# Attention with a position bias: score stacks of 64 rows for pairs of heads, two heads alternating on the halves of TensorE's rows, and all causal masks for the maxima on VectorE

## The chip, the cores and the metric

One core of a Trainium2 chip runs the whole program. Its engines run side by side and meet at semaphores: TensorE (PE; PEld is its weight load, which overlaps the matmuls), VectorE (DVE), ScalarE (ACT), GpSimd (POOL) and SyncE (SP), which here only issues DMAs. The metric is device time in microseconds, the median of repeated executions.

## What is computed

The input is `x` of 16 batches, 512 tokens and 256 features; there are 16 heads of 16 features. For each batch, with `xn` the layer norm of `x`:

```python
qkv = xn @ w_qkv.T + b_qkv                       # q, k, v of 16 heads
att = einsum('bhqd,bhkd->bhqk', q, k) / sqrt(16)
att = att + bias[h, q - k]                       # cosine features of the position, a constant for some heads
att = softmax(where(causal, att, -inf))
attn = einsum('bhqk,bhkd->bhqd', att, v) @ w_proj.T + b_proj
y    = bf16(fp8(bf16(xn)) @ fp8(kernel)) + bias_ffn
out  = x + attn + y
```

## The kernel before, in words

The fp32 operands are split into a rounded part (hi) and a rest (lo), and a product is hi·hi + hi·lo + lo·hi. For the scores this is done in one matmul, by stacking operands in rows: `STK` holds for each head 48 rows of q or k parts (three products of 16 features) and 48 rows of position features (again three products), and on the query side two more rows with the negated row maximum, in two parts. So a score tile is one matmul of 96 rows, and a transposed one, for the exponentials, one of 98.

A batch `b` is worked in four groups `g` of four heads. A group has 11 slots `k`. In slot `k` TensorE makes one bank of transposed scores of group `g` (`scores_T`, L586, banks `scoreT_a` to `_c`), which ScalarE turns into `probs` by exp (L801), and one bank of plain scores of the group two ahead (`scores`, L565, banks `score_a` to `_c`), of which VectorE takes the row maxima (`chunk_max`). Both kinds have three banks, so the matmuls of slot `k` wait until the bank of slot `k-3` is read. The bank widths: four slots of 512 columns, four of 384, then two slots that hold two heads of 256 columns each and one with four heads of 128. For the first eight slots VectorE adds the mask and takes the maximum in one custom operation on each bank (L882, followed by a read of the accumulator); for the last three TensorE has added the mask with bf16 matmuls (L561, L569), and VectorE only reduces (L878).

When a group's maxima are there, TensorE transposes them (`job_MT`, L543), ScalarE writes the rounded part (L730) and VectorE the rest (L887), and SP sends both rows into `STK`, before that group's transposed scores begin.

All other work is hung into the slots by tables of (group, slot), in `V_AT` to `MT_AT`: the v projection (V), transposes of the next batch's `xn` (T), its q and k projections (QK), the fp8 product (FF), the output projection (PJ), probabilities times values (PV, L597, with its output on 32 columns of the array for each head) and the maxima (MT). `DVE_LAG` says how many slots later VectorE reads the result. The eight PSUM banks are full: three and three, and `misc_a`, `misc_b` for all other jobs. GpSimd masks the diagonal blocks of `probs` (L1089). Each engine executes its own list strictly in this order.

## Time and profile before

| | before |
|---|---|
| median of 3 runs | 870.61 us (869.99 to 874.59) |
| the profiled execution, its own time | 878.46 us |
| its span | 876.7 us |
| mean granted TensorE clock | 0.967 of 2.4 GHz |
| PE busy | 812.9 us, 93% |
| DVE busy | 648.6 us, 74% |
| ACT busy | 553.7 us, 63% |
| POOL busy | 470.9 us, 54% |
| DMA: share of 16 engines, bytes | 49%, 90.68 MB |

The span is the time from the first to the last instruction in the trace. A matmul's row shows its whole latency, so neighbouring matmuls overlap in the rows; what one costs the engine is the distance from its start to the next one's start. The same holds for VectorE's rows, which overlap by some 0.08 us.

### The profile page before, as it was taken

Reading aid. Unit: us, or ns where it says so; the run is one execution under the profiler, and the core shown is the slowest. Engines: PE = TensorE matmul, PEld = TensorE weight load, DVE = VectorE, ACT = ScalarE, POOL = GpSimd, SP = SyncE. Lnnn points to the kernel's source line nnn. Section 1 sums busy time; section 2 is a strip of 40 time slices with the busy share of each in tenths; the row PEclk is TensorE's granted clock in tenths of the full one; section 3 lists DMA queues with packets and bytes.
Section 4 is the critical chain, followed back from the end, with each engine's and each line's share of the span. In section 5 each row is a group of like instructions: output and inputs, shape, how many; then the busy total and the mean of one; then the engine's idle time right before and its main releaser. Section 6 shows DMA issues by size and latency. Waiting matters only on the chain.

```text
span 876.7 us, 21490 instructions
## 1 busy us (share of the span) xinstructions
PE 812.9 (93%) x5934; PEld 594.9 (68%) x5936; DVE 648.6 (74%) x1660; ACT 553.7 (63%) x1097; POOL 470.9 (54%) x485
## 2 busy tenths in 40 slices
PE   6699999999999998999999999999999999999983
PEld 3376676768677776867667586766768677776762
DVE  5976587787778878777787777777787778877732
ACT  4165576666767666675776577566666757766571
POOL 8533645546564654646475464645546464655442
PEclk9698799999999999999999999989999999999996
DMA  7834534464554455355445535653464554445312
GB/s 190 157 80 84 107 78 80 122 109 105 111 118 95 99 114 101 99 110 127 98 87 125 89 99 110 128 100 62 125 109 102 111 121 95 99 88 103 74 45 80
DMA packets 72453, 90.68 MB, mean 103 GB/s; under 512 B 18160, under 2 KB 38256, under 8 KB 72432
## 3 DMA queue, kind: packets, MB, share of 16 engines
q1 hardware_dynamic: 71360, 88.92, 48.2%
q10 hardware_dynamic: 1072, 1.51, 0.8%
q8 instruction: 9, 0.15, 0.1%
q14 instruction: 12, 0.10, 0.0%
HBM read 18.81 MB, written 8.91 MB: 32 GB/s over the span
## 4 chain that ended last, share of the span: by engine, by line
PE 57%; DVE 12%; SPq 9%; issue 8%; DMA 6%; ACT 5%; DVEq 1%; POOL 1%; ACTq 0%; POOLq 0%
PE misc_b L493 10%; PE misc_b L597 9%; PE misc_a L493 8%; SPq L272 8%; PE scoreT_b L586 6%; PE scoreT_a L586 4%; PE score_c L565 4%; PE score_a L565 4%; DMA stacks<-neg_max_T 4%; PE score_b L565 4%; PE scoreT_c L586 3%; DVE row_max L878 2%; ACT qk_parts L726 2%; DVE score_c L882 2%; DVE qk_parts L866 1%
## 5 line engine op out<-in xcount | busy, mean ns | idle before, releaser
L1089 POOL TENSOR_SCALAR_AFFINE_SELECT probs<-probs 128x512 f32<-128x512 f32 x256 | 160.2, 635 | 320.1 <-ACT probs L801 319.9
L801 ACT ACTIVATE probs<-scoreT_a 128x512 f32<-128x512 f32 (+1 forms) x240 | 135.3, 564 | 89.9 <-PE scoreT_a L586 89.4
L801 ACT ACTIVATE probs<-scoreT_b 128x512 f32<-128x512 f32 (+1 forms) x240 | 134.5, 561 | 85.0 <-PE scoreT_b L586 85.0
L882 DVE CUSTOM_DVE_ANT_0 score_a<-score_a,causal_mask_q 128x512 f32<-128x512 f32 (+1 forms) x176 | 112.8, 641 | 86.2 <-PE score_a L565 86.0
L801 ACT ACTIVATE probs<-scoreT_c 128x512 f32<-128x512 f32 (+1 forms) x224 | 125.6, 561 | 47.8 <-PE scoreT_c L586 47.7
L882 DVE CUSTOM_DVE_ANT_0 score_b<-score_b,causal_mask_q 128x384 f32<-128x384 f32 (+1 forms) x176 | 112.7, 640 | 43.8 <-PE score_b L565 28.4
L597 PE MATMUL misc_b<-probs,v_ones 128*32 128x128 f32 (+3 forms) x1536 | 120.8, 457 | 0.0
L586 PE MATMUL scoreT_b<-stacks 98*128 98x128 f32 (+3 forms) x368 | 105.2, 343 | 14.8 <-DMA stacks<-neg_max_T 14.1
L565 PE MATMUL score_a<-stacks 96*128 96x512 f32 (+3 forms) x336 | 108.4, 363 | 3.9 <-DVE row_max L882 2.6
L586 PE MATMUL scoreT_a<-stacks 98*128 98x512 f32 (+3 forms) x336 | 108.4, 369 | 1.7 <-ACT probs L801 1.5
L565 PE MATMUL score_b<-stacks 96*128 96x128 f32 (+3 forms) x368 | 108.8, 349 | 0.2 <-DVE row_max L882 0.2
L882 DVE CUSTOM_DVE_ANT_0 score_c<-score_c,causal_mask_q 128x512 f32<-128x512 f32 (+1 forms) x160 | 101.6, 635 | 3.8 <-PE score_c L565 3.3
L597 PEld LDWEIGHTS misc_b<-probs,v_ones 128*32 128x32 f32 x1536 | 46.5, 114 | 79.9 <-issue 71.2
L565 PE MATMUL score_c<-stacks 96*128 96x512 f32 (+3 forms) x320 | 99.9, 354 | 0.7 <-DVE row_max L882 0.7
L586 PE MATMUL scoreT_c<-stacks 98*128 98x512 f32 (+3 forms) x320 | 98.0, 355 | 0.6 <-ACT probs L801 0.6
L586 PEld LDWEIGHTS scoreT_b<-stacks 98*128 98x128 f32 x368 | 61.8, 193 | 27.4 <-DMA stacks<-neg_max_T 16.4
L565 PEld LDWEIGHTS score_a<-stacks 96*128 96x128 f32 x336 | 63.8, 198 | 12.5 <-DVE row_max L882 8.2
L882 DVE DVE_READ_ACCUMULATOR2_ANT row_max<- 128x1 f32 x512 | 71.9, 141 | 0.0
L565 PEld LDWEIGHTS score_b<-stacks 96*128 96x128 f32 x368 | 67.5, 198 | 3.8 <-DVE row_max L882 0.7
L586 PEld LDWEIGHTS scoreT_a<-stacks 98*128 98x128 f32 x336 | 57.5, 194 | 13.1 <-issue 6.1
L1078 POOL TENSOR_TENSOR quant_work<-quant_work 128x1024 f32<-128x1024 f32 x16 | 38.0, 2374 | 50.5 <-DVE quant_work L928 50.5
L565 PEld LDWEIGHTS score_c<-stacks 96*128 96x128 f32 x320 | 60.8, 198 | 4.2 <-DVE row_max L882 2.0
(234 smaller groups left out, 1824.9 us busy)
## 6 DMA issues: line engine op xcount, KB each, us to landing
stacks<-qk_parts SPq DMA_DIRECT2D x502, 96.0 KB, 2.8
x_ring<-in_L_attn_x SPq DMA_DIRECT2D x16, 512.0 KB, 3.9
attn<-out_T SPq DMA_DIRECT2D x64, 128.0 KB, 2.6
xn<-recips SPq DMA_DIRECT2D x31, 256.0 KB
out<-x_ring SPq DMA_DIRECT2D x15, 512.0 KB, 3.0
stacks<-neg_max_T SPq DMA_DIRECT2D x128, 8.0 KB, 1.8
stacks<-probs SPq DMA_DIRECT2D x16, 96.0 KB, 3.3
denominators<-out_T SPq DMA_DIRECT2D x64, 8.0 KB
```

Source lines behind the costliest of these rows:

```text
L272: eng.dma_start(STK[0:K_QK, g, a, h, :].bitcast(F32), QKP[r:r + HD, g // 2, :, a, :].bitcast(F32)) \
L493: last = mm(o, l(ct), r(ct), start=(ct == 0 and i == 0), stop=(ct == CT - 1 and i == 2))
L565: last = mm(SB_[n % 3][:, o:o + w], STK[0:K_SCORE, g, 0, h, P * qt:P * qt + P], STK[0:K_SCORE, g, 1, h, 0:w], start=(qt != 0), stop=(qt >= ...
L586: last = mm(bank[:, w * i:w * i + w], STK[0:K_ALL, g, 1, h, P * j:P * j + P], STK[0:K_ALL, g, 0, h, P * j:T], start=True, stop=True)
L597: last = mm(bank[32 * i:32 * i + 32, P * j:T], VA[:, j, HU * g + i, :, :].rearrange("p d a -> p (d a)"), probs(g, j)[:, i, :], start=(j == ...
L726: A(qk_part(m, 0), misc_of("QK", m)[:, :].unsqueeze(1).broadcast_to([P, 2, T]), ACT.Identity, bias=BQ[:, bias:bias + 1]).then_inc(qh_ready, 1)
L801: A(probs(g, j)[:, h0:h0 + nh, :], STB[(SLOTS * g + k) % 3][:, 0:nh * WJ[j]] .rearrange("p (h n) -> p h n", h=nh), ACT.Exp).then_inc(exp_d ...
L866: V.scalar_tensor_tensor(out=qk_part(m, 1), in0=misc_of("QK", m)[:, :], scalar=BQ[:, bias:bias + 1], in1=qk_part(m, 0)[:, 0, :].bitcast(F3 ...
L878: V.tensor_reduce(MX[:, g % 2, h0:h0 + nh, qt], bank.rearrange("p (h w) -> p h w", h=nh), AX_X, ALU.max).then_inc(max_done, 1)
L882: V.tensor_tensor_reduce(bank, bank, CMQ[:, T - w:T], 1.0, LEAST, ALU.add, ALU.max, MX[:, g % 2, h0, qt:qt + 1]).then_inc(max_done, 1)
L1078: GP.tensor_tensor(QT, QT, QM, ALU.add).then_inc(qr_done, 1)
L1089: GP.affine_select(out=d, in_=d, compare_op=ALU.is_ge, fill=0.0, base=0, pattern=[[0, HU], [1, P]], channel_multiplier=-1).then_inc(mask_d ...
```

## The change

- **Stacks.** A head has 64 rows: three products of q and k parts, and one row of rounded position features for each of the 16 features (`ROWS = 4` in `QKP`). Two heads stand one above the other, in rows 0 to 63 and 64 to 127 of `STK`. One DMA moves a pair (512 KB), two a group, where there were eight.
- **Low parts.** The small products of the features, and for groups 0 and 1 the two rows of maxima, stand in `EXT` (34 rows a head), and the transposed scores of these two groups get a second matmul that adds them (L602). The plain scores, whose maxima only shift the exponents, leave the low parts out. In groups 2 and 3 the bias is a constant, its parts fill spare rows, and the maxima replace two rows of `STK`.
- **Order.** `in_turn` alternates the matmuls of `scores_T` and `scores` within a slot. The transposed scores are of head `k % 4`, the plain ones of head `k % 4 ^ 1`, so the two stand on different halves of the rows.
- **Slots.** A group has 12: the last four hold for one head the tiles of 256 and 128 columns. The job tables are set anew.
- **Maxima.** The masks on TensorE are gone; VectorE's custom operation does every tile. VectorE splits the maxima into two parts before the transpose (`max_parts`, two small operations), so that ScalarE alone evacuates the transposed maxima.
- GpSimd has three waits for its masks in a group instead of four, with as many operations. The setup makes the constant rows and the low features in another way.

```diff
-PRODS = 3
-K_QK = PRODS * HD
-K_SCORE = 2 * K_QK
-K_ALL = K_SCORE + 2
-SLOTS = 11
-CHUNKS = 11
+PAIRS = H // 2
+ROWS = 4
+EXTRA = 34
+SLOTS = 12
+CHUNKS = 12
...
-SLOT_PLAN = [(0, h, 1) for h in range(4)] + [(1, h, 1) for h in range(4)] + [(2, 0, 2), (2, 2, 2), (3, 0, 4)]
-LAST_SLOT = [3, 7, 9, 10]
-PE_MASKED = (0, 1)
-CHUNK_PLAN = [(3, h, 1) for h in range(4)] + [(2, h, 1) for h in range(4)] + [(1, 0, 2), (1, 2, 2), (0, 0, 4)]
-V_AT = [(0, 3), (0, 4)]
-T_AT = [(0, 5), (0, 7)]
-QK_AT = [(0, 10), (1, 1), (1, 6), (2, 5)]
-FF_AT = [(2, 7), (2, 8)]
-PJ_AT = [(3, 3), (3, 6)]
-PV_AT = [(1, 2), (2, 2), (3, 2), (0, 2)]
-MT_AT = [(0, 1), (1, 3), (2, 3), (3, 1)]
+LAST_SLOT = [3, 7, 11]
+QUERY_TILES = [(3,)] * 4 + [(2,)] * 4 + [(1, 0)] * 4
+V_AT = [(0, 5), (0, 7)]
+T_AT = [(0, 9), (0, 9)]
+QK_AT = [(0, 11), (1, 1), (1, 7), (2, 9)]
+FF_AT = [(2, 7), (2, 7)]
+PJ_AT = [(3, 5), (3, 9)]
+PV_AT = [(1, 3), (2, 3), (3, 3), (0, 3)]
+MT_AT = [(0, 1), (1, 5), (2, 5), (3, 1)]
 ACT_LAG = {"T": 0, "QK": 0, "FF": 0, "MT": 0}
-DVE_LAG = {"V": 0, "T": 1, "QK": 1, "PJ": 0, "MT": 1}
+DVE_LAG = {"V": 0, "T": 1, "QK": 1, "PJ": 0}
 OUT_AT = 3
 AH_AT = [(2, 1), (2, 2)]
-INVERT_AT, LAST_INVERT_AT, DIVIDE_AT = (0, 10), (3, 7), (1, 10)
-STATS_AT, NORM_AT = (2, 6), [(3, 5), (3, 6), (3, 7), (3, 9)]
+INVERT_AT, LAST_INVERT_AT, DIVIDE_AT = (0, 11), (3, 8), (1, 10)
+STATS_AT, NORM_AT = (2, 7), [(3, 5), (3, 6), (3, 7), (3, 10)]
...
-        STK = sb("stacks", [P, G, 2, HU, T], F32R)
+        STK = sb("stacks", [P, PAIRS, 2, T], F32R)
+        EXT = sb("low_features", [P, PAIRS // 2, 2, T], F32R)
...
-        QKP = sb("qk_parts", [P, 2, PRODS, 2, T], F32R)
+        QKP = sb("qk_parts", [P, 2, ROWS, 2, T], F32R)
...
+        def rows_of(h):
+            return slice(64 * (h % 2), 64 * (h % 2) + 64), h // 2
+        def max_rows(g, h):
+            o, u = 64 * (h % 2), (HU * g + h) // 2
+            if g < 2:
+                return EXT[o + 32:o + 34, u, 0, :].bitcast(F32)
+            return STK[o + 11:o + 16:4, u, 0, :].bitcast(F32)
+        def send_max(eng, g):
+            for h in range(HU):
+                eng.dma_start(max_rows(g, h), MTS[2 * TT * h:2 * TT * h + 2 * TT, g % 2, :].bitcast(F32)) \
+                    .then_inc(max_loaded[g], 16)
...
-                for a in range(2):
-                    for h in range(HU):
-                        stack_part(sp, g, h, a)
+                for u in (2 * g, 2 * g + 1):
+                    r = 32 * (u % 4)
+                    sp.dma_start(STK[:, u, :, :].bitcast(F32), QKP[r:r + 32, u // 4, :, :, :].bitcast(F32)) \
+                        .then_inc(stack_loaded[g], 16)
             def load_max(b, g):
                 sp.wait_ge(mts_ready, 4 * b + g + 1)
-                for part in range(2):
-                    sp.dma_start(STK[K_SCORE + part:K_SCORE + part + 1, g, 0, :, :].rearrange("o h n -> o (h n)").bitcast(F32),
-                                 MTS[:, g % 2, part, :].bitcast(F32)).then_inc(max_loaded[g], 16)
+                send_max(sp, g)
...
             def job_MT(b, g):
-                pe.wait_ge(max_done, ROW * b + SLOTS * (g + 1))
+                pe.wait_ge(mh_done, 4 * b + g + 1)
                 bank = misc("MT", (g - 1) % G, b if g else b - 1)
-                nc.tensor.transpose(bank[0:HU * TT, 0:P], MX[:, g % 2, :, :].rearrange("p h t -> p (h t)"),
+                nc.tensor.transpose(bank[0:HU * 2 * TT, 0:P],
+                                    MXP[:, g % 2, :, :, :].rearrange("p h i t -> p (h i t)").bitcast(F32),
                                     IDF[:, :]).then_inc(mt_ready, 1)
             def scores(b, g, c, early=False):
-                qt, h0, nh = CHUNK_PLAN[c]
-                w = P * (qt + 1)
                 n = CHUNKS * g + c
+                rows, u = rows_of(HU * g + (c % 4 ^ 1))
                 if c == 0:
-                    if isinstance(b, int) and b == 0:
-                        pe.wait_ge(feat_loaded[g], 16 * (2 * HU if g < 2 else HU))
-                    pe.wait_ge(stack_loaded[g], 128 * (b + 1))
-                if n >= 3:
+                    pe.wait_ge(stack_loaded[g], 32 * (b + 1))
+                if n >= 3 or not early:
                     pe.wait_ge(max_done, ROW * b + n - 2)
-                elif not early:
-                    pe.wait_ge(max_done, ROW * b - [1, 0, 2][n])
-                if qt == 0:
-                    mm(SB_[n % 3][:, :].rearrange("p (h w) -> p h w", h=nh), CMT[:, :],
-                       IDB[:, :].unsqueeze(1).broadcast_to([P, nh, P]), start=True, stop=False)
-                for i in range(nh):
-                    h, o = h0 + i, w * i
-                    last = mm(SB_[n % 3][:, o:o + w], STK[0:K_SCORE, g, 0, h, P * qt:P * qt + P],
-                              STK[0:K_SCORE, g, 1, h, 0:w], start=(qt != 0),
-                              stop=(qt >= 2 or (qt == 0 and i == nh - 1)))
-                    if qt == 1:
-                        last = mm(SB_[n % 3][:, o + P:o + w], CMT[:, :], IDB[:, :], start=False, stop=True)
-                last.then_inc(s_ready, 1)
+                o = 0
+                for qt in QUERY_TILES[c]:
+                    w = P * (qt + 1)
+                    last = mm(SB_[n % 3][:, o:o + w], STK[rows, u, 0, P * qt:P * qt + P], STK[rows, u, 1, 0:w],
+                              start=True, stop=True)
+                    o += w
+                    if qt == QUERY_TILES[c][-1]:
+                        last.then_inc(s_ready, 1)
+                    yield
             def scores_T(b, g, k, first):
-                j, h0, nh = SLOT_PLAN[k]
-                w = WJ[j]
+                n = SLOTS * g + k
+                rows, u = rows_of(HU * g + k % 4)
+                extra = slice(rows.start, rows.start + EXTRA)
                 if k == 0:
-                    pe.wait_ge(max_loaded[g], 32 * (b + 1))
-                n = SLOTS * g + k
-                if n >= 3:
+                    if isinstance(b, int) and b == 0 and g < 2:
+                        pe.wait_ge(feat_loaded[g], 64)
+                    pe.wait_ge(max_loaded[g], 64 * (b + 1))
+                if n >= 3 or not first:
                     pe.wait_ge(exp_done, ROW * b + n - 2)
-                elif not first:
-                    pe.wait_ge(exp_done, ROW * b - [1, 0, 2][n])
-                bank = STB[n % 3]
-                for i in range(nh):
-                    h = h0 + i
-                    last = mm(bank[:, w * i:w * i + w], STK[0:K_ALL, g, 1, h, P * j:P * j + P],
-                              STK[0:K_ALL, g, 0, h, P * j:T], start=True, stop=True)
-                last.then_inc(st_ready, 1)
+                tiles = [k // 4] if k < 8 else [2, 3]
+                o = 0
+                for j in tiles:
+                    bank = STB[n % 3][:, o:o + WJ[j]]
+                    o += WJ[j]
+                    last = mm(bank, STK[rows, u, 1, P * j:P * j + P], STK[rows, u, 0, P * j:T], start=True, stop=(g >= 2))
+                    if g < 2:
+                        yield
+                        last = mm(bank, EXT[extra, u, 1, P * j:P * j + P], EXT[extra, u, 0, P * j:T],
+                                  start=False, stop=True)
+                    if j == tiles[-1]:
+                        last.then_inc(st_ready, 1)
+                    yield
+            def in_turn(*streams):
+                streams = list(streams)
+                while streams:
+                    streams = [x for x in streams if next(x, streams) is not streams]
...
-            def max_hi(b, g):
+            def max_T(b, g):
                 act.wait_ge(mt_ready, 4 * b + g + 1)
-                A(MTS[:, g % 2, 0, :], misc_of("MT", (g - 1) % G)[0:HU * TT, 0:P], ACT.Copy, scale=-1.0).then_inc(mh_done, 1)
+                A(MTS[:, g % 2, :], misc_of("MT", (g - 1) % G)[0:HU * 2 * TT, 0:P], ACT.Copy, scale=-1.0).then_inc(mts_ready, 1)
...
             def chunk_max(b, g, c):
-                qt, h0, nh = CHUNK_PLAN[c]
-                n = CHUNKS * g + c
-                w = P * (qt + 1)
-                bank = SB_[n % 3][:, 0:nh * w]
-                if qt in PE_MASKED:
-                    dve.wait_ge(s_ready, ROW * b + n + 1)
-                    V.tensor_reduce(MX[:, g % 2, h0:h0 + nh, qt], bank.rearrange("p (h w) -> p h w", h=nh),
-                                    AX_X, ALU.max).then_inc(max_done, 1)
-                else:
-                    wait_alone(dve, (x_loaded, 16), (s_ready, ROW * b + n + 1))
-                    V.tensor_tensor_reduce(bank, bank, CMQ[:, T - w:T], 1.0, LEAST, ALU.add, ALU.max,
-                                           MX[:, g % 2, h0, qt:qt + 1]).then_inc(max_done, 1)
-            def max_T(b, g):
-                dve.wait_ge(mh_done, 4 * b + g + 1)
-                V.scalar_tensor_tensor(out=MTS[:, g % 2, 1, :], in0=misc_of("MT", (g - 1) % G)[0:HU * TT, 0:P],
-                                       scalar=-1.0, in1=MTS[:, g % 2, 0, :].bitcast(F32),
-                                       op0=ALU.mult, op1=ALU.subtract).then_inc(mts_ready, 1)
+                n, h, o = CHUNKS * g + c, c % 4 ^ 1, 0
+                wait_alone(dve, (x_loaded, 16), (s_ready, ROW * b + n + 1))
+                for qt in QUERY_TILES[c]:
+                    w = P * (qt + 1)
+                    bank = SB_[n % 3][:, o:o + w]
+                    o += w
+                    last = V.tensor_tensor_reduce(bank, bank, CMQ[:, T - w:T], 1.0, LEAST, ALU.add, ALU.max,
+                                                  MX[:, g % 2, h, qt:qt + 1])
+                last.then_inc(max_done, 1)
+            def max_parts(b, g):
+                dve.wait_ge(max_done, ROW * b + CHUNKS * (g + 1))
+                V.tensor_copy(MXP[:, g % 2, :, 0, :], MX[:, g % 2, :, :]).then_inc(mx_hi, 1)
+                dve.wait_ge(mx_hi, 4 * b + g + 1)
+                V.tensor_tensor(MXP[:, g % 2, :, 1, :], MX[:, g % 2, :, :], MXP[:, g % 2, :, 0, :].bitcast(F32),
+                                ALU.subtract).then_inc(mh_done, 1)
...
```

In the rows of the order below, as in the whole text, names after the arrow are what is read. First TensorE at the start of group 0, before: slot 0, then slot 1, transposed scores and plain scores of whole 98 and 96 rows.

```order
L586 MATMUL scoreT_a<-stacks 128x512
L554 REGISTER_ALU
L557 REGISTER_ALU
L565 MATMUL score_b<-stacks 128x512
L586 MATMUL scoreT_b<-stacks 128x512
L557 REGISTER_ALU
L565 MATMUL score_c<-stacks 128x512
```

The same place in the changed kernel: a third matmul in each slot of groups 0 and 1. The rows used go lower, upper, lower in the even slots and upper, lower, upper in the odd ones.

```order
L599 MATMUL scoreT_a<-stacks 128x512
L570 REGISTER_ALU
L572 REGISTER_ALU
L576 MATMUL score_a<-stacks 128x512
L602 MATMUL scoreT_a<-low_features 128x512
L593 REGISTER_ALU
L599 MATMUL scoreT_b<-stacks 128x512
L572 REGISTER_ALU
L576 MATMUL score_b<-stacks 128x512
L602 MATMUL scoreT_b<-low_features 128x512
```

What moved: the extra matmul stands where there was none, and every neighbour is on the other half. In groups 2 and 3 there is no L602. Now VectorE at the end of group 0, before: three plain reductions, with jobs between.

```order
L878 TENSOR_REDUCE row_max<-score_a 128x2
L859 REGISTER_ALU
L860 TENSOR_TENSOR xnT_lo<-misc_b,xnT_hi 128x512
L877 REGISTER_ALU
L878 TENSOR_REDUCE row_max<-score_b 128x2
L877 REGISTER_ALU
L878 TENSOR_REDUCE row_max<-score_c 128x4
L902 REGISTER_ALU
L903 RECIPROCAL denominators_inv<-denominators 128x64
```

And the last two slots there in the changed kernel, behind two more of the kind:

```order
L905 ISA score_b,row_max<-score_b,causal_mask_q 128x256
L905 ISA row_max 128x1
L905 ISA score_b,row_max<-score_b,causal_mask_q 128x128
L905 ISA row_max 128x1
L886 ISA
L887 TENSOR_TENSOR xnT_lo<-misc_a,xnT_hi 128x512
L886 REGISTER_ALU
L887 TENSOR_TENSOR xnT_lo<-misc_b,xnT_hi 128x512
L309 REGISTER_ALU
L905 ISA score_c,row_max<-score_c,causal_mask_q 128x256
L905 ISA row_max 128x1
L905 ISA score_c,row_max<-score_c,causal_mask_q 128x128
```

What moved: a group ends in eight custom operations where three reductions stood, and both `xnT_lo` stand together ahead of the last slot. Two small operations of `max_parts` (L912, L914) follow.

## Rows read from the trace of the kernel before

**Rows 1.** Windows by batch: PE, PEld, DVE, ACT, POOL busy, PEclk, DMA share.

```profile
407.30:457.80 50.50, 48.64 (x370) 36.22 (x368) 39.58 (x103) 34.34 (x69) 28.41 (x29) 1.00 0.50 107
457.80:510.10 52.30, 50.08 (x369) 36.68 (x368) 39.76 (x103) 34.42 (x68) 28.40 (x29) 0.97 0.49 103
...
560.60:614.70 54.10, 51.72 (x369) 37.32 (x368) 39.84 (x103) 34.39 (x69) 28.41 (x29) 0.94 0.48 99
```

**Rows 2.** Windows of the batch at 407.3, one for each group.

```profile
407.30:422.20 14.90, 14.82 (x114) 11.79 (x113) 10.99 (x27) 9.14 (x19) 8.61 (x9) 1.00 0.47 113
422.20:433.70 11.50, 10.84 (x80) 7.79 (x79) 8.90 (x24) 8.04 (x16) 6.82 (x7) 1.00 0.56 121
433.70:445.80 12.10, 11.29 (x86) 7.95 (x85) 9.54 (x30) 9.08 (x18) 4.78 (x5) 1.00 0.48 87
445.80:457.80 12.00, 11.70 (x96) 8.69 (x94) 10.15 (x26) 8.09 (x17) 8.21 (x10) 1.00 0.52 105
```

**Rows 3.** Timeline of TensorE (start us, duration us), matmuls of four widths.

```profile
411.55 0.28 PE L493 MATMUL misc_a<-w_qkvT_hi,xnT_hi 128*128 128x256 f32 x1
411.67 0.28 PE L493 MATMUL misc_a<-w_qkvT_lo,xnT_hi 128*128 128x256 f32 x1
...
418.09 0.64 PE L586 MATMUL scoreT_b<-stacks 98*128 98x128 f32 x4
...
421.40 0.40 PE L586 MATMUL scoreT_a<-stacks 98*128 98x512 f32 x1
421.64 0.39 PE L565 MATMUL score_b<-stacks 96*128 96x512 f32 x1
...
440.32 0.34 PE L586 MATMUL scoreT_b<-stacks 98*128 98x384 f32 x1
440.50 0.34 PE L565 MATMUL score_a<-stacks 96*128 96x384 f32 x1
```

**Rows 4.** Timeline of TensorE around one PV job.

```profile
408.35 0.40 PE L565 MATMUL score_a<-stacks 96*128 96x512 f32 x1
408.68 2.36 PE L597 MATMUL misc_b<-probs,v_ones 128*32 128x512 f32 x32
410.97 0.50 PE L586 MATMUL scoreT_a<-stacks 98*128 98x512 f32 x1
```

**Rows 5.** Timeline of VectorE in groups 2 and 3.

```profile
440.99 0.57 DVE L882 CUSTOM_DVE_ANT_0 score_a<-score_a,causal_mask_q 128x384 f32<-128x384 f32 x1 [1.02 <-PE score_a L565]
...
441.67 0.75 DVE L866 SCALAR_TENSOR_TENSOR qk_parts<-misc_b,b_qk,qk_parts 128x512 fp32r<-128x512 f32 x1
442.34 1.40 DVE L850 BATCH_NORM_STATS2 bn_six<-x_ring 128x6 f32 x4
...
444.05 0.57 DVE L882 CUSTOM_DVE_ANT_0 score_b<-score_b,causal_mask_q 128x384 f32<-128x384 f32 x1
...
446.94 0.69 DVE L925 TENSOR_SCALAR xn<-quant_work 128x1024 int32<-128x1024 int32 x1
...
448.80 0.69 DVE L882 CUSTOM_DVE_ANT_0 score_a<-score_a,causal_mask_q 128x512 f32<-128x512 f32 x1
...
449.41 0.73 DVE L882 CUSTOM_DVE_ANT_0 score_b<-score_b,causal_mask_q 128x512 f32<-128x512 f32 x1
450.06 0.14 DVE L882 DVE_READ_ACCUMULATOR2_ANT row_max<- 128x1 f32 x1
...
453.45 0.60 DVE L882 CUSTOM_DVE_ANT_0 score_b<-score_b,causal_mask_q 128x384 f32<-128x384 f32 x1
453.97 0.14 DVE L882 DVE_READ_ACCUMULATOR2_ANT row_max<- 128x1 f32 x1
...
455.87 0.69 DVE L878 TENSOR_REDUCE row_max<-score_b 128x2 f32<-128x512 f32 x1
```

**Rows 6.** Waits: engine, line, what it waited for, us in total, times, longest.

```profile
PE scoreT_b L586 <- DMA stacks<-neg_max_T: 14.1, 16, 1.5
```

**Rows 7.** Window just before the granted clock fell in the batch at 457.8.

```profile
481.20:484.60 3.40, 2.35 (x18) 2.06 (x17) 3.34 (x6) 1.93 (x6) 1.85 (x3) 1.00 0.50 107
```

220 lines of the change are left out of this document (119 added, 101 removed).

## The prediction

> **What bounds the kernel now.** I read the windows by batch first, to find a batch that stands for all. With the clock at 1.00 a batch takes 50.5 us, with PE busy 48.6, DVE 39.6, ACT 34.3 and POOL 28.4 [rows 1]. Cut at the groups, the same batch shows PE busy for 14.8 of 14.9 us in group 0 and 10.8 to 11.7 of 11.5 to 12.1 in the others [rows 2]. A busy PE may be latency alone, so I took distances between starts from TensorE's timeline: 0.24 us for 512 columns, 0.18 for 384, 0.12 for 256 and (0.64 - 0.28) / 3 = 0.12 for 128 [rows 3]. From 256 columns up that is 0.46 ns a column; 128 columns cost as much as 256, so there the weight load behind each matmul sets the pace, at about 0.12. Both kinds of score matmuls have in a group 4 matmuls of each width: 2 x 4 x (0.24 + 0.18 + 0.12 + 0.12) = 5.3 us, 21 a batch. The rest of PE's work is PV, 4 x 2.3 (408.68 to 410.97) [rows 4], 24 matmuls of 512 columns for q and k (5.6) and 48 of 256 for v and the projection (5.7), some 1.8 for FF and T, and about 1 for masks: 44 with the scores, and the remaining 6 of the 50.5 are switches and waits. So TensorE bounds the batch, VectorE stands 20% below it.
>
> **TensorE's side of the change.** Whether two matmuls on different rows run at once, no row of before shows: all use rows from 0 up. The nearest is PV, where four matmuls go to different columns of the array: 32 of them, f32, last 2.36 us [rows 4]. They stream 8 x (512 + 384 + 256 + 128) = 10,240 columns, 4.7 us at 0.46 ns if one by one, in half that time even counting each f32 operand once. So parts of the array do work at once. For rows the bounds are none at all and a full halving; I take the halving, as the nearest row points there. The Trainium skill, "TensorE: Matmul & The Clock Gate", section Part 3, states the same for rows, with 3.07 times for four row tiles; by its figure a pair would come out nearly halved too.
>
> The pitch of weight loads remains. If loads stay one by one at 0.12, groups 2 and 3 cost in a slot 0.24 (two of 512), 0.24 (two of 384, by the loads), and 0.48 (four loads): 4 x 0.96 = 3.8 us instead of 5.3 plus masks. Groups 0 and 1 have three matmuls instead of two: 0.36, 0.36 and 0.72, so 4 x 1.44 = 5.8: nothing is gained there. If loads overlap too, it is 4 x (0.24 + 0.18 + 0.18) = 2.4 and 3.6. I take loads one by one, since the 128-column row shows that pace; the other is the low bound. PE's work in a batch falls from 44 to 44 - 1 - 21.1 + 2 x 3.8 + 2 x 5.8 = 41 us, or 34 with overlapping loads.
>
> Against it speaks a rule that the rows allow a price for. From the score at 408.35 to PV is 0.33 us where 0.24 would be the pitch [rows 4], so a switch costs about 0.09. Now only PV's four jobs switch; if half rows against whole rows is such a switch, the 18 places of jobs have two each: 36 x 0.09 = 3.2 us, 2.5 more than now. The Trainium skill, "TensorEngine Tiling (Array Packing)", section Key Properties, says that a change of tiling mode drains the array. I count the cost in the high bound, where TensorE is late.
>
> **VectorE's side.** Distances of starts: custom maximum of 512 columns 0.61 when something else stands before it, 0.65 behind another one; of 384, 0.52; a reduction 0.69 less the overlap of 0.08, 0.61 [rows 5]. 256 and 128 columns do not occur; by the step of 0.13 for 128 columns they are 0.39 and 0.26, and I take that (bounds 0.14, what a read of the accumulator shows, and 0.52). Slots: 0.65, 0.52 and 0.65, so 4 x 1.82 = 7.3 us a group instead of 4 x 1.17 + 3 x 0.61 = 6.5. `max_parts` has two operations that wait on their own engine: I take 0.45 (each at least the 0.14 of the smallest row, each with a wait of the like), against 0.2 for the operation removed. Other jobs: QK_lo 0.67 each (441.67 to 442.34), statistics 1.7 (to 444.05), the quantiser 1.86 (446.94 to 448.80) [rows 5]; v, T_lo, projection result 0.6 each like the reduction, division 1.2, inversion 0.55 (estimates by size: 1024 columns are twice, 64 few). Groups 0 to 3: 7.75 + 3.0, + 3.2, + 2.4, + 3.1 = 42.7 us a batch, where it was about 39. VectorE's work is now above TensorE's 41, and neither can be followed without waits.
>
> **The walk.** A matmul's start to the start of its maximum is 0.5 us (440.50 to 440.99) [rows 3, 5]. PE may be three banks ahead, no more.
> - Group 3, t from the first maximum: maximum 0.6, quantiser to 2.5, three maxima to 4.4. PE issues slot 3 at 0.9, then PV to 3.5 and slot 4, in time. Maxima 4 and 5 to 5.5; PJ (12 x 0.12 = 1.4, PE 4.0 to 5.5) is read from 5.7 to 6.3; four maxima to 8.6; the second PJ ends at 8.8, read to 9.7; slots 10 and 11 and `max_parts` to 11.4. Now 12.0.
> - Group 2: PV ends at 3.3, slot 4 can be read at 4.0, VectorE has been out of work since 2.6; then its own work to 11.4. Now 12.1.
> - Group 1: PV again (0.9 idle), QK before slot 8 (another 1.0), the rest VectorE's own: 12.1. Now 11.5.
> - Group 0: after slot 3 PE has PV, four slots of 0.36 and two V of 1.4, read with no lag: VectorE idles some 3 us; then T and slots 8 to 11 at 0.72, with two T_lo ahead of the last maximum: 14.7. Now 14.9 [rows 2].
>
> The sum is 49.6 against 50.5: 0.9 us a batch. 15 batches have this form (the last is half without plain scores): 13.5 us.
>
> **Costs taken at nothing.** ACT: three exponentials of 512 become four of 384, hidden, ACT has 16 us free [rows 1]. DMA: four MB of stacks a batch instead of three, share 0.50 now [rows 1]; a stack is sent some ten slots before its use. SP issues 6 DMAs for stack and maxima in a group where it issued 10, so the wait of group 2's first slot for its maxima (14.1 us in 16 times) [rows 6] can go: up to 0.9 a batch, inside the walk's group 2. If the larger DMAs delayed the maxima, that 0.9 would stay. The start and end I leave even: two more maxima slots (1.2 us) against fewer feature DMAs.
>
> **From the profiled execution to the median.** 876.7 - 13.5 = 863.2 of span, 865 as its own time; it ran 7.9 above the median of before, 870.61, so the median comes to 857.
>
> **The rivals.**
> 1. *As forecast* (34%): pairs run at once, the three banks and the jobs without lag couple the engines; 48.8 to 50.0 a batch: 846 to 864.
> 2. *A looser coupling* (22%): weight loads of the two halves overlap as well, group 0 loses 4 x (1.44 - 0.9) = 2.2 us of PE, groups 1 to 3 fall to VectorE's 10.9, 10.2 and 10.9 plus one PV gap of about 1: 46 to 48.7 a batch, 805 to 845. For it: PV's many loads take no visible time in rows 4. Against it: VectorE's rows don't shrink.
> 3. *Nothing moves* (12%): the walk is 0.6 to 1.1 short, for instance because half of the 2.5 us of switches falls on groups 0 and 1: 866 to 875.
> 4. *The clock* (20%), slower. The granted clock fell in the batch at 457.8 (0.97, 52.3 us) and at 560.6 (0.94, 54.1 us) [rows 1], 1.8 and 3.6 us dearer. In the stretch ahead PE was busy 2.35 of 3.4 us while DVE was busy 3.34 [rows 7]: TensorE sat waiting for VectorE. With pairs TensorE waits so in groups 2 and 3 of each batch. From one short fall in every second batch the 0.9 is gone; with one in each it is +0.9 x 15, 884, with a longer one 910.
> 5. *The rows do not run at once* (12%), slower: PE loses the masks (1) and gains 2 x 4 x 0.66 = 5.3 for the low parts, so +4.3, or +6.8 with all switches: 54.8 to 57.3 a batch, 935 to 973.
>
> **How the numbers follow.** The likeliest case gives 857. Case 2 reaches to 805; below 818 I leave out 5%. Above I take case 4 up to 895 and leave out its end and case 5, together 15%. A measurement of this kernel tells about 0.5%, 4 us, from no change; faster by more is 1 and 2, 56%; within, 12%; slower 4 and 5, 32%.
>
> **What would show it.** In the changed profile: starts of L599 and the L576 behind it some 5 to 20 ns apart in groups 2 and 3 (case 5: 0.24); starts of four matmuls of 256 and 128 in 0.48 us (case 2: 0.24); L905 at 0.39 and 0.26 for the small tiles and DVE busy near 43 us a batch; PE waiting for `row_max` in groups 2 and 3 and DVE waiting for PE after each PV; groups of 14.7, 12.1, 11.4 and 11.4 us; granted clock at 1.00 in most batches (case 4: well below). The prediction fails if small custom operations cost as much as the 384 one, (0.13 + 0.26) x 16 = 6 us a batch, or if PE's column pitch doubles when both halves stream.

## The result, and the profile after

The changed kernel takes 1044.8 us (median, 1044.3 to 1047.3) where the one before takes 871.1: 1.199 times as long, 95% interval 1.195 to 1.203. The forecast was 857 us, with 15% left for more than 895; even its dearest case ended at 973. The page of the profiled execution:

```profile
span 1042.7 us, 22828 instructions
PE 886.2 (85%) x6131; PEld 530.7 (51%) x6131; DVE 737.7 (71%) x2553; ACT 563.6 (54%) x1162; POOL 479.6 (46%) x490
PEclk9578888888888898888889888888988888888887
```

Against [rows 1], the windows of one batch, 417.5 to 479.2, cut at its four groups (same columns as in [rows 2]):

```profile
417.50:437.00 19.50, 16.48 (x121) 10.51 (x121) 13.98 (x46) 9.32 (x21) 10.11 (x10) 0.84 0.45 116
437.00:450.60 13.60, 11.27 (x93) 7.13 (x92) 10.15 (x33) 8.16 (x18) 6.62 (x6) 0.98 0.58 125
450.60:464.40 13.80, 13.44 (x82) 6.71 (x79) 9.54 (x43) 9.11 (x20) 3.85 (x4) 0.75 0.50 92
464.40:479.20 14.80, 11.96 (x93) 8.47 (x92) 12.01 (x42) 8.14 (x19) 8.71 (x10) 0.88 0.45 81
sum 61.70, PE 53.15 PEld 32.83 DVE 45.68 ACT 34.73 POOL 29.30; mean PE 13.29 PEld 8.21 DVE 11.42 ACT 8.68 POOL 7.32
```

Read two things: the clock column, 0.75 to 0.98 where [rows 2] had 1.00 in all groups, and PE's idle time, 3.0, 2.3, 0.4 and 2.8 us, 8.5 a batch, where the batch of [rows 1] had 1.9. Windows of six batches in a row, of before and then of after, give the account that the rest of this text uses:

```profile
255.70:560.60 304.90, 292.93 (x2209) 217.61 (x2209) 237.50 (x613) 205.99 (x409) 170.47 (x174) 0.99 0.51 106
```

```profile
295.10:663.30 368.20, 320.81 (x2282) 192.65 (x2280) 273.41 (x948) 209.27 (x433) 175.69 (x174) 0.86 0.50 105
```

Idle is length less PE busy. A stretch of mean clock c loses about (1 - c) of its length, since at the lower level (1.2 GHz) work takes nearly twice as long (a PV job below: 4.49 us and 2.36); what is left is PE busy at full clock. Per batch: before 50.8 = 48.3 work + 2.0 idle + 0.5 clock; after 61.4 = 44.9 work + 7.9 idle + 8.6 clock. TensorE's work shrank, by 3.4 us on this account. Waits cost 5.9 more and the clock 8.1 more. (The clock has two digits in such a row, and the work worked out so differs between kernels with equal matmuls, 43.6 us in e8_stack_act and 47.6 in e13_moved_old_sp. So waits and clock are clear, and the 3.4 us of work are within that spread.)

Where TensorE waits, in the whole execution, from the view of the waits (us in total, times, longest):

```profile
PE misc_a L561 <- DVE row_max_parts L914: 42.7, 30, 2.9
PE scoreT_a L599 <- DMA stacks<-neg_max_T: 32.1, 17, 2.1
PE misc_a L511 <- DVE xnT_lo L887: 26.4, 15, 1.8
...
ACT out_T L813 <- PE misc_b L621: 157.2, 48, 4.3
DVE score_b L905 <- PE score_b L576: 144.9, 72, 4.1
```

The first three make 101 us, 6.3 a batch. The second is the wait of [rows 6], 32.1 now instead of 14.1; the others were next to nothing. The last two rows are engines that wait for TensorE, mostly while it works on PV. Of the four PV jobs of the batch shown, two run at the lower clock, with 4.05 and 4.49 us, and two at the full one, with 2.36 as in [rows 4]. TensorE's timeline has this one:

```profile
452.29 0.79 PE L576 MATMUL score_a<-stacks 64*128 64x512 f32 x1 [0.15 <-DVE row_max L905]
453.01 4.49 PE L621 MATMUL misc_b<-probs,v_ones 128*32 128x512 f32 x32
```

In this batch the clock falls four times, and each time behind a wait of over a microsecond that had ended 0.7 to 1.5 us before: for the split maxima (1.25 us, group 0), for the input's low part (1.77, group 0), for the maxima's DMAs (2.05, group 2), and at 472.83 for ScalarE's exponentials (1.44, at the end of group 3). A fifth, 1.40 us for the split maxima in group 3, ended at 466.15, and the clock stayed up behind it. Windows from there to the fall, and behind it:

```profile
464.00:475.10 11.10, 8.09 (x70) 5.14 (x71) 10.09 (x32) 6.06 (x15) 7.29 (x9) 1.00 0.61 109
475.20:478.50 3.30, 3.30 (x21) 3.08 (x21) 1.52 (x8) 1.68 (x5) 1.32 (x2) 0.50 0.00 0
```

In four of the six batches it is the other way round: the wait for exponentials is missing, and the clock falls behind the transpose of group 3.

The two halves of the rows do run at once. TensorE's timeline, slots of 384 columns and then of 256 and 128:

```profile
302.10 0.34 PE L602 MATMUL scoreT_b<-low_features 34*128 34x384 f32 x1
302.10 0.33 PE L599 MATMUL scoreT_c<-stacks 64*128 64x384 f32 x1
302.27 0.34 PE L602 MATMUL scoreT_c<-low_features 34*128 34x384 f32 x1
...
307.02 0.33 PE L576 MATMUL score_a<-stacks 64*128 64x256 f32 x1
307.08 0.22 PE L599 MATMUL scoreT_a<-stacks 64*128 64x128 f32 x1
307.15 0.27 PE L602 MATMUL scoreT_a<-low_features 34*128 34x128 f32 x1
```

Two matmuls of 384 columns start in the same 10 ns and the next two 0.17 us on; the narrow ones follow at 0.06, half of the 0.12 of [rows 3], so weight loads of the two halves overlap too. What it costs to switch between half and whole rows shows around a V job, whose matmuls use all 128 rows. TensorE's timeline, after and then before:

```profile
424.69 0.34 PE L576 MATMUL score_c<-stacks 64*128 64x384 f32 x1
424.95 0.39 PE L511 MATMUL misc_a<-w_qkvT_hi,xnT_hi 128*128 128x256 f32 x1
...
426.56 0.44 PE L599 MATMUL scoreT_a<-stacks 64*128 64x384 f32 x1
...
426.84 0.34 PE L602 MATMUL scoreT_a<-low_features 34*128 34x384 f32 x1
```

```profile
411.55 0.28 PE L493 MATMUL misc_a<-w_qkvT_hi,xnT_hi 128*128 128x256 f32 x1
...
412.97 0.34 PE L586 MATMUL scoreT_b<-stacks 98*128 98x384 f32 x1
413.16 0.34 PE L565 MATMUL score_c<-stacks 96*128 96x384 f32 x1
```

The job spans 1.61 us instead of 1.42, and the pairs of scores at its two ends take 0.27 and 0.28 instead of 0.17. That is 0.4 us for two switches between half and whole rows, 0.2 each.

Last, the end of a group: GpSimd's timeline, VectorE's, TensorE's, and then VectorE's groups of instructions:

```profile
464.63 1.22 POOL L1116 TENSOR_SCALAR_AFFINE_SELECT probs<-probs 128x512 f32<-128x512 f32 x2 [3.91 <-ACT probs L829]
```

```profile
465.33 0.56 DVE L912 CAST row_max_parts<-row_max 128x16 fp32r<-128x16 f32 x1
465.92 0.18 DVE L914 TENSOR_TENSOR row_max_parts<-row_max,row_max_parts 128x16 fp32r<-128x16 f32 x1
466.13 0.70 DVE L905 CUSTOM_DVE_ANT_0 score_a<-score_a,causal_mask_q 128x512 f32<-128x512 f32 x1
```

```profile
466.15 0.28 PE L561 MATMUL misc_a<-ident_f,row_max_parts 128*32 128x128 f32 x1 [1.40 <-DVE row_max_parts L914]
```

```profile
L914 DVE TENSOR_TENSOR row_max_parts<-row_max,row_max_parts 128x16 fp32r<-128x16 f32 x64 | 31.1, 485 | 2.2
L912 DVE CAST row_max_parts<-row_max 128x16 fp32r<-128x16 f32 x64 | 29.1, 454 | 2.2
```

The last two rows are the groups of VectorE's instructions in the whole execution (busy us, mean ns). From 465.33 to 466.13 the two operations of `max_parts` keep VectorE from the next group's first maximum, and TensorE stands for 1.40 us in front of the transpose. The first of them takes 0.56 us and ends just behind GpSimd's masking (465.85); the second, behind it, takes 0.18. Of the 128 operations of `max_parts` in this trace 74 took over 0.3 us, and each of the 74 ended 18 to 31 ns after a GpSimd instruction that had begun before it. Where GpSimd was idle they took 0.17 and 0.18 us.

### The profile page after: what moved, and what is told of

Its sections match the earlier page's. It is cut to its first block, busy times and chain, and to the rows that moved or that the text cites. A ratio compares the mean times of both kernels' runs of the same rounds, so it can differ in the third digit from the quotient of the medians.

```text
span 1042.7 us, 22828 instructions
## 1 busy us (share of the span) xinstructions
PE 886.2 (85%) x6131; PEld 530.7 (51%) x6131; DVE 737.7 (71%) x2553; ACT 563.6 (54%) x1162; POOL 479.6 (46%) x490
## 4 chain that ended last, share of the span: by engine, by line
PE 66%; DVE 11%; issue 8%; DMA 4%; SPq 4%; ACT 3%; POOL 2%; DVEq 1%; ACTq 0%; POOLq 0%
PE misc_b L621 16%; PE misc_b L511 10%; PE misc_a L511 9%; PE scoreT_a L599 5%; PE scoreT_b L599 4%; PE misc_a L621 4%; PE scoreT_c L599 4%; SPq L303 3%; PE score_a L576 3%; ACT probs L829 2%; DVE score_c L905 2%; PE score_c L576 2%; DVE row_max L905 2%; DVE xnT_lo L887 2%; DMA stacks<-neg_max_T 2%
## 5 line engine op out<-in xcount | busy, mean ns | idle before, releaser
L905 DVE CUSTOM_DVE_ANT_0 score_b<-score_b,causal_mask_q 128x384 f32<-128x384 f32 (+3 forms) x320 | 164.7, 531 | 145.9 <-PE score_b L576 144.9
L905 DVE CUSTOM_DVE_ANT_0 score_c<-score_c,causal_mask_q 128x256 f32<-128x256 f32 (+3 forms) x384 | 171.9, 475 | 34.8 <-PE score_c L576 34.3
L905 DVE CUSTOM_DVE_ANT_0 score_a<-score_a,causal_mask_q 128x512 f32<-128x512 f32 (+3 forms) x320 | 172.3, 555 | 18.0 <-PE score_a L576 14.2
L599 PE MATMUL scoreT_a<-stacks 64*128 64x512 f32 (+3 forms) x320 | 126.6, 411 | 44.4 <-DMA stacks<-neg_max_T 32.1
L829 ACT ACTIVATE probs<-scoreT_c 128x384 f32<-128x384 f32 (+1 forms) x256 | 132.9, 519 | 35.0 <-PE scoreT_c L602 31.9
L829 ACT ACTIVATE probs<-scoreT_b 128x384 f32<-128x384 f32 (+1 forms) x256 | 132.2, 517 | 19.8 <-PE scoreT_b L599 18.1
L576 PE MATMUL score_a<-stacks 64*128 64x512 f32 (+3 forms) x320 | 127.7, 431 | 9.1 <-DMA stacks<-qk_parts 5.4
L599 PE MATMUL scoreT_b<-stacks 64*128 64x384 f32 (+3 forms) x320 | 121.3, 400 | 4.6 <-ACT probs L829 4.6
L599 PE MATMUL scoreT_c<-stacks 64*128 64x256 f32 (+3 forms) x384 | 116.7, 337 | 5.4 <-ACT probs L829 5.4
L576 PE MATMUL score_b<-stacks 64*128 64x384 f32 (+3 forms) x320 | 119.8, 407 | 0.9 <-DVE row_max L905 0.2
```

The costliest lines, as they stand in the source:

```text
L576: last = mm(SB_[n % 3][:, o:o + w], STK[rows, u, 0, P * qt:P * qt + P], STK[rows, u, 1, 0:w], start=True, stop=True)
L599: last = mm(bank, STK[rows, u, 1, P * j:P * j + P], STK[rows, u, 0, P * j:T], start=True, stop=(g >= 2))
L829: A(probs_slot(g, k), STB[(SLOTS * g + k) % 3][:, 0:w], ACT.Exp).then_inc(exp_done, 1)
L905: last = V.tensor_tensor_reduce(bank, bank, CMQ[:, T - w:T], 1.0, LEAST, ALU.add, ALU.max, MX[:, g % 2, h, qt:qt + 1])
```

## The experiments

**The theories.** (A) The side-by-side work is quick but leaves TensorE with short waits in the open, for VectorE and for DMAs; the chip answers with the lower clock, which doubles the loss. (B) VectorE's load is the bound: masks and maxima of all tiles. (C) The maxima come late because of SP's queue or the DMA engines. (D) Running the halves side by side is worth little. Times are medians; "ratio" is to the kernel before in the same runs (its medians were 871 to 877), with the 95% interval. The windows are of six batches, columns as above.

### Is running side by side worth anything: e6_same_half

```diff
-                rows, u = rows_of(HU * g + k % 4)
+                rows, u = rows_of(HU * g + HEADS[k % 4])        # HEADS = [0, 2, 1, 3]
```

The same in `scores`, `chunk_max` and `probs_slot`.

> The kernel after, with only the order of heads changed to 0, 2, 1, 3, the same for the scores and the transposed scores: neighbours in TensorE's queue then stand on the same half of the rows, and nothing can run side by side save at two places in a slot of four. All waits, VectorE, ScalarE, GpSimd and the DMAs are the same. A batch has 51,200 columns of score matmuls; by the after trace (0.21 us for 512) they take 21 us one after the other, and 11 to 12 side by side. If alternation is worth that and the clock is unchanged, this kernel takes 1160 to 1200. If running side by side leaves TensorE so thin that the lower clock and the waits take the gain back, this one is granted a higher clock (0.93 or more against 0.847) and takes 1030 to 1090.

1150.7 us, ratio 1.321 (1.316 to 1.325), clock 0.844:

```profile
319.10:731.80 412.70, 380.73 (x2281) 243.53 (x2281) 275.60 (x951) 218.34 (x434) 176.70 (x174) 0.84 0.44 93
```

Work 52.5 us a batch instead of 44.9: the halves give 7.6 a batch, 106 us in all, and (D) is out. (The expectation counts 0.21 us for 512 columns; the rows have 0.24, before and after.) The clock is as low as with pairs, so side-by-side matmuls are not what lowers it. Not every fall here has a long wait just ahead: at 355.3 us it came behind 15 us in which TensorE's only wait was of 0.3 us. What brought it was not found.

### The clock: e1_dup, e7_fill, e11_fill_three

e1_dup runs each plain score matmul twice. The other two add matmuls of no use ahead of a wait:

```diff
+                fill(FILL[0], bank)              # 6; e11: only where g < 2
                 pe.wait_ge(mh_done, 4 * b + g + 1)
...
+                        fill(FILL[1], bank)      # 8
                     pe.wait_ge(xl_ready, 2 * (b + 1))
...
+                        fill(FILL[2], STB[n % 3])  # 9; e11: only where g == 2
                     pe.wait_ge(max_loaded[g], 64 * (b + 1))
```

> The changed kernel (1044.8 us, granted clock 0.847), with every plain score matmul issued twice into the same bank. Pure extra work for TensorE, 64 matmuls a batch. Theory C: about 17 us of each 61 us batch run at half clock, because TensorE idles between pairs, and that is most of the loss. Then more columns hold the clock up (0.95 or more) and the time falls although there is more work, to 900 to 990. Theory W: the loss is the waits that the new order makes (about 6.7 us more idle TensorE in a batch), and the clock only follows. Then the extra 2 to 5 us of matmuls a batch add up: 1045 to 1110, clock about as it was.

> The kernel after, with matmuls of no use at the three places where TensorE waits longest, ahead of the wait and into a bank that is free: 6 bf16 matmuls of 512 columns ahead of each transpose of the maxima, 8 ahead of the q and k projections, 9 ahead of the first transposed scores of each group (1.3 to 1.9 us each at full clock; 11 us of such work a batch where waits are now 8 us). If the lower clock is what TensorE's idle places bring about, and costs 8 us of a batch, the clock goes from 0.847 to 0.93 or more, and the kernel takes 980 to 1035 in spite of the additional work. If the waits alone are the cost, and the clock follows from something else, the clock stays under 0.88 and the time is 1045 to 1090.

> The kernel after, with matmuls of no use at only those four places in a batch where its trace shows a wait of over 1 us (6 ahead of two transposes of maxima, 8 ahead of the first projection, 9 ahead of the third group's transposed scores: 29 matmuls, 6.2 us a batch instead of e7_fill's 14.5). The waits stay about as long as they are and are only filled, so that what is gained is the clock's share alone. If the clock rises as in e7_fill (0.974), a batch takes 46.7 plus 6.2 to 8.5 us, 53 to 55.5, and the kernel 905 to 950. If it needed all of e7_fill's work to rise, the clock stays at or below 0.90 and the time over 1000.

e1_dup 1053.5 us, ratio 1.202 (1.195 to 1.209), clock 0.887. e7_fill 1042.8, ratio 1.196 (1.192 to 1.200), clock 0.974. e11_fill_three 965.9, ratio 1.103 (1.097 to 1.109), clock 0.962. Windows of e1_dup, e7_fill and e11_fill_three:

```profile
304.00:672.60 368.60, 331.42 (x2666) 214.14 (x2667) 273.86 (x949) 212.97 (x433) 175.67 (x174) 0.91 0.50 105
```

```profile
300.40:667.50 367.10, 345.33 (x2654) 205.04 (x2688) 274.60 (x949) 213.37 (x433) 175.96 (x175) 1.00 0.50 105
```

```profile
282.60:619.90 337.30, 314.43 (x2456) 193.40 (x2456) 274.88 (x949) 208.84 (x434) 175.92 (x174) 0.99 0.54 114
```

Work that stands beside other work (e1_dup) brings the clock up in part, and its own 4.8 us a batch eat what comes back (idle 6.2, clock 5.5). Work in the waits brings it to 1.00. In e7_fill its 14.5 us a batch eat all that the clock and the waits gave (idle 3.6). With e11_fill_three's 6.2 the batch is 56.2: idle 3.8, clock 0.6, and 51.8 - 6.2 = 45.6 of the kernel's own work. Same jobs, more work, and 79 us less: in this kernel the lower clock follows from the waits of over a microsecond, and costs at least those 79. (In e2_jobs and e17_hi_act_no_fill below, as in e6_same_half, some of the falls had no such wait just ahead, so it is not the only way to a fall.) That leaves 95 us of the 174.

### VectorE's masks in the kernel before: e4_before_dve, e5_before_both_masks

e4: in the kernel before, the two narrow kinds of tile get VectorE's masking instruction, and TensorE's mask matmuls go. e5: the same, with TensorE's mask matmuls kept.

```diff
-                    dve.wait_ge(s_ready, ROW * b + n + 1)
-                    V.tensor_reduce(MX[:, g % 2, h0:h0 + nh, qt], bank.rearrange("p (h w) -> p h w", h=nh),
-                                    AX_X, ALU.max).then_inc(max_done, 1)
+                    wait_alone(dve, (x_loaded, 16), (s_ready, ROW * b + n + 1))
+                    for i in range(nh):
+                        tile = bank[:, w * i:w * i + w]
+                        last = V.tensor_tensor_reduce(tile, tile, CMQ[:, T - w:T], 1.0, LEAST, ALU.add, ALU.max,
+                                                      MX[:, g % 2, h0 + i, qt:qt + 1])
+                    last.then_inc(max_done, 1)
```

> The kernel before with one part of the change alone: no masks by TensorE, VectorE's custom operation on each tile of 256 and 128 columns too. VectorE gains 16 x (0.35 + 0.25) - 12 x 0.6 = 2.4 us a batch, TensorE loses 1.0. If TensorE is what bounds and VectorE's load is hidden: 855 to 872. If VectorE is already felt in groups 2 and 3: 875 to 895, and the clock falls in more batches than two of sixteen.

> The kernel before, with VectorE's masking instruction on every tile as in e4_before_dve, but with TensorE's mask matmuls kept too (the two narrow kinds of tile are masked twice, which changes no maximum). It differs from e4_before_dve only in TensorE having its old work. If e4_before_dve lost its 60 us because TensorE, with its mask matmuls gone and more waits, was granted the lower clock (0.912 against 0.97 or so), this kernel comes back to 880 to 905 with a clock of 0.95 or more. If it lost them because VectorE's additional instructions stand in the ring of three score banks, so that TensorE waits for them whatever else it does, this kernel takes 930 to 950, with VectorE as long busy as in e4_before_dve.

e4 937.0 us, ratio 1.067 (1.058 to 1.076), clock 0.912; e5 907.4, ratio 1.041 (1.034 to 1.048), clock 0.957. Windows of e4, then of e5:

```profile
274.80:603.10 328.30, 302.20 (x2088) 212.26 (x2088) 253.40 (x927) 209.06 (x410) 171.01 (x174) 0.93 0.47 98
```

```profile
262.20:580.40 318.20, 299.78 (x2209) 218.09 (x2208) 254.24 (x925) 208.49 (x408) 170.72 (x174) 0.98 0.48 101
```

So VectorE's masking, put alone into the kernel before, costs 4.1 to 6.7%. VectorE is as busy in both (42.2 and 42.4 us a batch), and the kernel in which TensorE does more is 2.5% (22 us) quicker: taking matmuls away made the wait for VectorE longer and the clock lower (idle 4.4 and clock 3.8 a batch against 3.1 and 1.1). The rest, 4.1%, comes with VectorE's 2.8 us more a batch, the only thing that e5 changes. My expectation for e4 had 895 us as the dearer end.

### Queues and DMAs: e3_max_act, e8_stack_act

e3: the maxima's DMAs are issued by ScalarE behind `max_T`. e8: the stacks' DMAs go from ScalarE's queue, the maxima stay on SP.

```diff
+                act.wait_ge(mts_ready, 4 * b + g + 1)      # e3
+                send_max(act, g)
...
+                            if (g, k) == (1, 5):            # e8, and at (0, 0), (2, 0), (3, 1)
+                                act.wait_ge(ql_ready, 4 * (b + 1) + 2)
+                                load_stack(b + 1, 0)
```

> The changed kernel with the four small DMAs of a group's maxima issued by ScalarE, right behind its copy, instead of by SyncE behind the 1 MB of stacks. A third theory, D, is the DMA queue: the four issues took 2.7 to 6.5 us on SyncE and TensorE waited 32.1 us in 17 times for them at the start of group 2. If that is so the wait goes: 2 us a batch, 1005 to 1020, and the clock rises a little. If the transfer itself is slow whatever the queue, or ScalarE's 2.4 us of issuing a group is felt: 1045 to 1080.

> The kernel after, with the DMAs of the stacks (two of 512 KB a group) issued from ScalarE's queue, so that in SP's queue the four small DMAs of the maxima don't stand behind them. ScalarE has slack. If the maxima are late because of the queue (4.8 to 6.5 us instead of 1.2), TensorE's wait of 2 us at the start of a group's transposed scores goes, once or twice a batch, and the kernel takes 1000 to 1030. If the DMA engines themselves are what is shared, the maxima take as long from their own queue and the time stays within 5 us of 1045; if ScalarE's issues hold its exponentials back, it is over 1060.

e3 1158.2 us, ratio 1.324 (1.314 to 1.334): the four small issues now block the exponentials (the waits of e3):

```profile
ACT probs L828 <- issue: 169.0, 44, 6.4
```

e8 1052.4, ratio 1.207 (1.203 to 1.211), 8 us worse. Issues of the maxima on SP's queue in the kernel after, and then in e8, where no stack stands before them on that queue (the second stack of the pair is issued by ScalarE at 449.50):

```profile
441.13 1.24 SPq L335 DMA_DIRECT2D stacks<-qk_parts  x2
444.01 4.79 SPq L303 DMA_DIRECT2D stacks<-neg_max_T  x4
```

```profile
449.50 0.63 ACTq L798 DMA_DIRECT2D stacks<-qk_parts  x1
```

```profile
450.54 5.33 SPq L303 DMA_DIRECT2D stacks<-neg_max_T  x4
```

Four DMAs of 4 KB take 4.8 us to issue here (2.7 to 6.5 in the four groups of the batch), and 5.3 from a queue without stacks while the stacks' 1 MB is under way in the other. So it isn't the order in SP's queue alone; that the two queues share something behind them is a guess that no run tests. Part of (C) holds, and neither change of queue mends it.

### Moving the jobs: e2_jobs, e9_moved, e13_moved_old_sp, e14_moved_stack_act, e10_moved_fill

```diff
-MT_AT = [(0, 1), (1, 5), (2, 5), (3, 1)]
+MT_AT = [(0, 4), (1, 5), (2, 5), (3, 4)]    # e2; e9, e10, e13, e14: (1, 2) in second place
-T_AT = [(0, 9), (0, 9)]
+T_AT = [(0, 8), (0, 8)]
-QK_AT = [(0, 11), (1, 1), (1, 7), (2, 9)]
+QK_AT = [(1, 0), (1, 1), (1, 7), (2, 9)]    # not in e2
```

e9 and e10 also put `load_max(b, 2)` ahead of `load_stack(b + 1, 0)` on SP; e13 doesn't; e14 sends stacks as e8 does, one of them a slot earlier. e10 is e9 with 14 of the useless matmuls.

> The changed kernel with the transposes of the maxima moved from slot 1 to slot 4 of groups 0 and 3, and the transposes of xn from slot 9 to slot 8 of group 0. In slot 1 TensorE waits for VectorE's max_parts (42.7 us in 30 times), at the first q and k matmul for xnT_lo (26.4 us in 15). Theory W: these waits go, 3 to 4 us a batch, 980 to 1000. Theory C: the same waits are what lets the clock fall, so more than their own length comes back, 940 to 980, with the clock above 0.9; if the waits only move elsewhere, 1030 to 1045.

> The kernel after, with its jobs placed so that what TensorE waited for is ready: the transposes of the maxima three slots later in groups 0 and 3 and three earlier in group 1, the transposes of the normalised input one slot earlier, the first q and k projection one slot later, and in SP's queue the maxima of group 2 ahead of the next batch's stacks. TensorE's jobs, their number and shapes are the same. In e7_fill a batch without its 14.5 us of additional matmuls is 46.7 us of TensorE at nearly full clock. If the waits of the after trace (1.25, 1.77, 2.05, 1.4 us a batch) and the lower clock that goes with them are the loss, this kernel needs 49 to 54 us a batch and takes 860 to 940. If VectorE is behind it (44 us busy of each batch, in a ring of three banks), the waits come back at other places, as waits of scores for row maxima, and it takes 990 to 1035.

> e9_moved without the swap in SP's queue (the next batch's stacks again ahead of the maxima of group 2); the jobs stand as in e9_moved. If the wait of 3.65 us for the stacks, and the stretch at the lower clock behind it, are what made e9_moved slow, this kernel loses them, gets back at most the 2 us wait for the maxima, and takes 990 to 1035. If it is the moved jobs (the first two projections close together at the start of group 1), the wait for the stacks stays and it takes 1055 to 1080.

> The jobs as in e9_moved, SP's order as in the kernel after, but the stacks' DMAs issued from ScalarE's queue as in e8_stack_act (one slot earlier at group 1). Neither the maxima nor the stacks then stand behind one another in a queue. If the place in the queue is what makes them late, no wait for either is left and the kernel takes 960 to 1010. If they share the DMA engines, one of the two waits (1.5 us or more a batch) stays and it takes 1020 to 1060.

> e9_moved with 3 to 4 matmuls of no use ahead of the transposes of the maxima of two groups, of the first projection and of the third group's transposed scores (14 in a batch, 3.0 us at full clock). If e9_moved still shows stretches at the lower clock behind short waits, this one is 5 to 40 us faster than e9_moved. If e9_moved is already without them, it is 20 to 45 us slower.

e2 1034.2 us, ratio 1.180 (1.173 to 1.187). e9 1070.9, 1.228 (1.224 to 1.233). e13 1047.8, 1.202 (1.198 to 1.207). e14 1090.0, 1.251 (1.243 to 1.258). e10 1064.4, 1.221 (1.217 to 1.225). The waits of e2, then of e9, then of e13:

```profile
PE score_a L576 <- DVE row_max L905: 33.5, 48, 2.7
```

```profile
PE score_a L576 <- DMA stacks<-qk_parts: 60.7, 16, 5.5
```

```profile
PE score_a L576 <- DVE row_max L905: 34.0, 45, 2.7
```

In e9 each of the three waits of the after trace was gone and another stood in its place: the maxima went first and the stacks came late; without that swap (e13) 23 us come back, so it was the dearer part, but the moves alone still gain nothing over the kernel after. With stacks from ScalarE (e14) they are late as well (65.7 us of waits). In e2 the waits at the transposes are gone for a gain of 11 us. They became a wait of the next group's scores for VectorE's maxima: what is late is VectorE, at the end of the group. My expectations for e9 (860 to 940, or up to 1035), for e14 (at most 1060) and for e3 (at most 1080) were wrong.

### VectorE, its load or its place: e15, e16, e17, e12, e18

e15 is e2_jobs with useless matmuls only ahead of the first projection (6) and of group 2's transposed scores (9). e16 is e15 with the first of the two operations of `max_parts` on ScalarE at the start of the next group, and the second on VectorE behind its second maximum:

```diff
-                            if k == CHUNKS - 1:
-                                max_parts(nb, ng)
+                        if k == 1 and not (first and g == 0) and not (last and g == 3):
+                            max_lo(*((b, g + 1) if g < 3 else (b + 1, 0)))
...
+                A(MXP[:, g % 2, :, 0, :], MX[:, g % 2, :, :], ACT.Copy).then_inc(mx_hi, 1)
```

e17 is e16 without any useless matmul. e12 is e11_fill_three, and e18 is e17, with the maximum of half a tile (both leave out the maxima of the other half, and serve only to take work from VectorE):

```diff
-                    last = V.tensor_tensor_reduce(bank, bank, CMQ[:, T - w:T], 1.0, LEAST, ALU.add, ALU.max,
+                    half = bank[:, 0:w // 2]
+                    last = V.tensor_tensor_reduce(half, half, CMQ[:, T - w:T - w // 2], 1.0, LEAST, ALU.add, ALU.max,
```

> The placement of e2_jobs, where no transpose of maxima is waited for, with matmuls of no use only ahead of the first projection (6) and of the third group's transposed scores (9): 3.2 us a batch instead of e11_fill_three's 6.2. If it is the idle places alone that bring the lower clock, it stays at 0.95 or more and the kernel takes 900 to 945. If TensorE's thin stretches (ends of groups, narrow tiles, VectorE the slower) lower it too, the clock is 0.88 to 0.93 and the time 960 to 1010.

> e15_jobs_fill_two, with the first of the two operations that split the maxima moved from VectorE to ScalarE at the start of the next group (0.17 to 0.66 us each, four a batch). If VectorE's load is a cost here, it is 5 to 25 us faster than e15_jobs_fill_two. If what counts is when the maxima are sent, it is within 5 us or slower, since the second operation comes two slots later.

> e16_hi_on_act without any matmul of no use, that is e2_jobs (1034 us) with the first operation that splits the maxima moved to ScalarE. If VectorE's late maxima at the end of each group are what starts the waits and the lower clock, the move gives here about what it gave with the filled waits (61 us), and the kernel takes 965 to 990. If the two waits that stay (the projection for the low part of the input, the third group for its maxima) are enough to bring the lower clock back, it takes 1000 to 1030.

> e11_fill_three with VectorE's masking and maximum taken over only the first half of each tile's keys (so the maxima of the other half are left out; the work of all other engines is the same). That takes some 10 us a batch from VectorE's 44. If VectorE's load holds TensorE up even with the clock restored, this kernel is 25 to 60 us faster than e11_fill_three. If TensorE alone then sets the pace, it is within 10 us of it.

> e17_hi_act_no_fill with VectorE's masking and maximum over only the first half of each tile's keys (so the maxima of the other half are left out), some 10 us a batch less for VectorE; all other work as in e17. e11_fill_three had 45.9 us of TensorE in a batch beside its waits and useless matmuls, against 50.4 us for a whole batch before. If VectorE is what keeps the change from paying, this kernel comes to 46 to 50 us a batch, 805 to 870 us. If waits on DMA and ScalarE and the lower clock stay, it takes 900 us or more.

| | us | ratio (95%) | clock |
|---|---|---|---|
| e15_jobs_fill_two | 1005.1 | 1.156 (1.149 to 1.162) | 0.911 |
| e16_hi_on_act | 944.0 | 1.084 (1.079 to 1.088) | 0.954 |
| e17_hi_act_no_fill | 958.2 | 1.093 (1.086 to 1.101) | 0.904 |
| e12_fill_half_max | 937.8 | 1.073 (1.068 to 1.078) | 0.961 |
| e18_hi_act_half_max | 946.8 | 1.082 (1.076 to 1.088) | 0.903 |

e15 does half of e11_fill_three's useless work and is 39 us slower: with the transposes moved away, the wait that e11 filled stands open at the next group's scores (37.3 us for `row_max`, 54 times). Windows of e17, then of e18:

```profile
279.10:613.60 334.50, 302.87 (x2282) 187.50 (x2282) 273.73 (x925) 212.47 (x458) 175.73 (x174) 0.93 0.54 115
```

```profile
279.00:606.10 327.10, 292.66 (x2282) 184.49 (x2280) 208.98 (x925) 211.80 (x457) 178.12 (x174) 0.94 0.55 118
```

Two small operations at the end of each group, out of VectorE's way, are worth 76 us (e17 against e2) or 61 (e16 against e15), where I had expected 5 to 25 from less load. VectorE isn't less busy for it: 273.73 us in the six batches of e17, 271.42 in those of e2, since the second operation, at its new place, takes 1134 ns on average instead of 514. The tile's row in one batch of e16 (ns, least, median, most), and the longest of the four on VectorE's timeline, with GpSimd's ahead of it:

```profile
L938 DVE TENSOR_TENSOR row_max_parts<-row_max,row_max_parts x4: 168/1082/1974, 402.5 to 440.9; 128x16 fp32r<-128x16 f32 x4
```

```profile
440.73 2.13 POOL L1146 TENSOR_TENSOR xnT_bf<-xnT_bf,b_ffn 128x1024 bf16<-128x1024 bf16 x1
```

```profile
440.92 1.97 DVE L938 TENSOR_TENSOR row_max_parts<-row_max,row_max_parts 128x16 fp32r<-128x16 f32 x1
```

It ends 0.03 us behind GpSimd's instruction, like the long ones of the kernel after. Ten microseconds a batch less for VectorE, on top, give only 11 us (e18) or 28 (e12). So it is mainly the place of the work and not its amount, and (B) as I had put it falls. How much is due to each of the two operations wasn't tried apart.

In e18 a batch is still 54.5 = 45.5 work + 5.7 idle + 3.3 clock. No version of the changed kernel beats the one before: the nearest that computes everything is e16, 8.4% slower.

## Why the prediction was wrong

**The halves run at once: right, and better than taken.** The low bound, weight loads overlapping, is what the trace shows. The forecast of case 5 (0.24 between the two starts) is refuted, and e6_same_half prices alternation at 106 us. A pair of 384 columns takes 0.17 us where one took 0.18 [rows 3]. The Trainium skill, "TensorE: Matmul & The Clock Gate", section Part 3, has matmuls on different row tiles run at once; the trace agrees for halves, with that 0.17.

**TensorE's work: a term mis-sized.** 41 us forecast, from 44; 44.9 measured, from 48.3. That both fall by some 3 is luck. The loads overlap, and with them the sum was 34, a fall of 10. What a switch costs was left to the high bound, and at half its size: 0.09 is what shows on one side of a switch. V's two jobs span 1.61 to 1.64 us where they spanned 1.42 before, and with the pairs of scores at their ends two switches cost 0.4. The Trainium skill, "TensorEngine Tiling (Array Packing)", section Key Properties, has the array drained at a change of tiling mode; the trace agrees, with that 0.2 a switch. By an estimate from these rows the 14 jobs that did not switch before cost 14 x 0.4 = 5.6 us a batch more. With the 34, and the 4.3 by which the list of jobs fell short of the measured work before, that makes 43.9.

**VectorE's durations: right, their price not.** Starts are 0.34 to 0.38 and 0.25 us apart for 256 and 128 columns (0.39 and 0.26 forecast); 45.6 us busy a batch, with forecast starts adding to 42.7. But the walk let VectorE's added work cost next to nothing, and in the kernel before it costs 4.1% by itself (e5_before_both_masks).

**`max_parts` at 0.45 us: the step that failed first.** It takes 0.94 us on average (0.45 and 0.49), up to 1.7, since more than half of its operations end only with a GpSimd instruction; where both are free of it they take 0.35 together. And I put it in the walk as a length of VectorE's work only. It stands where it does most harm: ahead of the next group's first maximum, with TensorE's transpose right behind it at slot 1. 42.7 us of waits in the after trace end with it, and moving its two operations is worth 76 us.

**"A stack is sent some ten slots before its use" and fewer issues on SP: wrong.** I counted DMAs and not what each holds up. A stack is 512 KB now and lands in 7.8 us, where one part of a stack before was 96 KB and took 2.8; the maxima take 4.8 us to issue. The wait of [rows 6] went from 14.1 to 32.1 us instead of going away. e8 and e9 show that neither another queue nor another order mends it.

**The clock (case 4): right in kind, far too small.** I took one fall in a batch, at 1.8 us or, longer, at 3.6. The batch shown has four stretches at 1.2 GHz, 17 us together, and a mean batch loses 8.6. I had placed the cause in TensorE's waits for the scores' maxima in groups 2 and 3; it lies in waits of over a microsecond at other places (two in group 0, one at the start of group 2, one or two in group 3), none of them in my walk. [rows 7] showed the pattern, and I should have put the same question to each place where a wait was added. By e11_fill_three the clock's price is at least 79 us.

**The walk as a whole** gave groups of 14.7, 12.1, 11.4 and 11.4 us; measured 19.5, 13.6, 13.8 and 14.8. It followed two engines and three banks. The path from maximum to split, transpose, ScalarE, SP, DMA and back to TensorE wasn't walked at all, and the three largest waits are on it or at the like path of the input's low part. Of the 174 us, 79 at least are the clock's and 76 `max_parts`' place (the two overlap, since filling the waits and removing them mend part of the same). What the rest consists of, the 73 us from e16's 944.0 to the 871 of before, is open in part: in e16 a batch has 3.2 us of useless matmuls, and 3.7 idle instead of 2.0.

## What to carry to other kernels

Before taking work from the engine that is the bound, list what waits for whom through a whole cycle, small operations and DMAs included; a 0.5 us operation at the end of one group, with the next group's first maximum behind it, cost far more here than one between two maxima. Where the bound engine gets shorter jobs, its waits come into the open, and the clock can more than double them (here 5.9 us of waits and 8.1 of clock a batch): price a change by its waits, not by its work. Filling the waits with useless matmuls is a quick test of how much of a loss is the clock's. And a cost read at one edge of a job is half a cost: read the distances on both sides of it.

## What was not expected of the hardware

- Matmuls of 64 and 34 rows on two halves start within 10 ns of each other, and loads of weights overlap as well: 0.06 us between narrow matmuls, 0.12 before.
- More work in the waits gave 79 us back (e11_fill_three), while doubling the score matmuls beside other work raised the clock less (0.847 to 0.887) and gave no time back (e1_dup, 1053.5 us).
- A 128 x 16 subtraction on VectorE takes 168 ns to 1974 ns, median 1082, in one batch of e16_hi_on_act, the same instruction each time. The long ones end with a GpSimd instruction: in the kernel after, 74 of 128 such operations took over 0.3 us, and all 74 ended 18 to 31 ns behind one. No run takes GpSimd's work away, so this is the trace's reading and not a test.
- A switch between half and whole rows costs TensorE 0.2 us, half of it inside the neighbouring scores.
- Four 4 KB DMAs took 5.3 us to issue from a queue in which no stack stood, while 1 MB was under way from another engine's queue.
